# A residual moved into the sum over experts, and a multiplication by gamma moved to GpSimd

## What is computed

```python
mixed = jnp.einsum('bnsed,bnse->bnsd', out.reshape(b, nh, s, ne, d), gs)
resid = sx[jnp.arange(nh), jnp.arange(nh)]
hn = layernorm(mixed + resid, ln_g, ln_b)
f_n = jnp.transpose(hn, (0, 2, 1, 3)).reshape(b, s, h)
fx = f_n.reshape(b, s, nh, d)
...
hx = layernorm(hx + fx, fnorm_g, fnorm_b)
fout = hx.reshape(b, s, h)
fg = jax.nn.softmax(fout @ fgate_w.T, axis=-1)
return (fout.reshape(b, s, nh, d) * fg[..., None]).reshape(b, s, h)
```

## Time and profile before

| what | value |
|---|---|
| median of 3 runs | 1426.47 us (1425.58 to 1429.7) |
| the profiled execution | 1430.59 us |
| its span in the profile | 1428.8 us |
| TensorE busy | 1322.5 us (93%) |
| VectorE busy | 1045.4 us (73%) |
| GpSimd busy | 737.2 us (52%) |
| ScalarE busy | 808.5 us (57%) |
| mean granted TensorE clock | 0.962 of full speed |

### The profile page before, as it was taken

The page is one execution under the profiler, slowest core; times in us unless marked ns, Lnnn a source line. Parts: engine busy times, 40 slices in busy tenths (PEclk is TensorE's granted clock), DMA queues, the critical chain, the costliest instruction groups (busy, mean ns, idle before and its releaser), DMA issues.

```text
span 1428.8 us, 46875 instructions
## 1 busy us (share of the span) xinstructions
PE 1322.5 (93%) x16052; PEld 944.7 (66%) x16052; DVE 1045.4 (73%) x3414; ACT 808.5 (57%) x2178; POOL 737.2 (52%) x1502
## 2 busy tenths in 40 slices
PE   1699999999899999999999999984899999999996
PEld 1455555555556666666666666653698998999996
DVE  8356766666636788888888888876577776588886
ACT  4355555555456566666666666643455454566663
POOL 6575555555424555555555555554454545455440
PEclk9999999999899999999999999995699999899998
DMA  3000000000000000000000000000000000000000
GB/s 154 1 2 1 0 0 0 0 0 0 2 1 2 2 2 0 0 0 0 0 0 0 0 0 0 0 2 1 0 1 0 0 0 1 2 7 11 5 11 13
DMA packets 6981, 7.93 MB, mean 6 GB/s; under 512 B 6272, under 2 KB 6272, under 8 KB 6784
## 3 DMA queue, kind: packets, MB, share of 16 engines
q1 hardware_dynamic: 6912, 7.02, 1.5%
HBM read 5.48 MB, written 1.54 MB: 5 GB/s over the span
## 4 chain that ended last, share of the span: by engine, by line
PE 74%; DVE 10%; issue 5%; ACT 3%; POOL 2%; DVEq 0%; ACTq 0%; POOLq 0%
PE bank_one L1397 12%; PE bank_five L954 6%; PE bank_five L1503 4%; PE bank_quad L1484 4%; PE bank_quad L1458 4%; PE bank_quad L933 3%; PE bank_pair L2290 3%; PE bank_pair L987 3%; PE bank_pair L1448 2%; PE bank_pair L1985 2%; PE bank_five L1507 2%; PE bank_quad L2280 2%; PE bank_five L1937 2%; PE bank_pair L1443 2%; PE bank_pair L1444 2%
## 5 line engine op out<-in xcount | busy, mean ns | idle before, releaser
L1382 POOL TENSOR_SCALAR_AFFINE_SELECT ex_pT<-ex_pT 128x512 f32<-128x512 f32 (+1 forms) x256 | 127.0, 519 | 178.4 <-ACT ex_pT L1623 172.0
L2360 ACT ACTIVATE mo_hT<-bank_quad,mo_b 128x188 f32<-128x188 f32 x256 | 86.1, 418 | 70.3 <-PE bank_quad L2280 70.1
L1686 DVE TENSOR_REDUCE ex_negmaxA<-bank_pair 128x4 bf16<-128x512 f32 x128 | 88.6, 692 | 32.5 <-PE bank_pair L1444 30.2
L1603 ACT ACTIVATE ex_pT<-bank_quad 128x496 f32<-128x496 f32 x128 | 74.8, 584 | 64.7 <-PE bank_quad L1487 63.7
L1924 POOL TENSOR_TENSOR ta_kk<-ta_ext 94x320 f32<-94x320 f32 x64 | 60.2, 959 | 95.2 <-DVE ta_qkn L2128 95.2
L1080 ACT ACTIVATE al_pT<-bank_quad 128x496 f32<-128x496 f32 x128 | 75.1, 588 | 49.5 <-PE bank_quad L937 49.3
L1372 POOL TENSOR_TENSOR ex_zrstd<-ex_zvar,neg_half 94x16 f32<-94x16 f32 x34 | 100.6, 2959 | 2.8
L2290 PE MATMUL bank_pair<-wsb,mo_hT 128*94 128x64 f32 x1024 | 96.0, 247 | 4.1 <-DVE mo_weighted L2422 3.3
L2290 PEld LDWEIGHTS bank_pair<-wsb,mo_hT 128*94 128x94 f32 x1024 | 90.2, 163 | 6.5 <-DVE mo_weighted L2422 4.0
L1184 DVE RECIPROCAL al_rec<-bank_five 128x188 f32<-128x188 f32 x64 | 84.7, 1323 | 3.4 <-PE bank_five L954 3.4
L862 POOL TENSOR_SCALAR_AFFINE_SELECT al_pT<-al_pT 128x512 f32<-128x512 f32 (+1 forms) x128 | 63.4, 519 | 41.0 <-ACT al_pT L1080 27.7
(11 more groups left out here) (365 smaller groups left out, 4004.2 us busy)
## 6 DMA issues: line engine op xcount, KB each, us to landing
tok_xin<-x_t SPq DMA_DIRECT2D x4, 760.0 KB, 6.9
wsb<-weights SPq DMA_DIRECT2D x1, 2308.0 KB, 13.7
out<-stream SPq DMA_DIRECT2D x16, 94.0 KB
tok_par<-tok_w SPq DMA_DIRECT2D x1, 4.5 KB, 1.6
```

The lines of the kernel that those rows point to most:

```text
L1382: nc.gpsimd.affine_select(out=view, in_=view, compare_op=ALU.is_ge, fill=0.0, base=shift, pattern=[[0, NH], [1, cols]], channel_multiplier ...
L1686: red(negmaxA[e % 2][:, D::32], R[:, 0, :].rearrange("p (n s) -> p n s", n=NH), AX.X, ALU.max, negate=True)\
L2360: nc.scalar.activation(hT[p][:, e, :], HB[e // 2 % 2][:, (e % 2) * N:(e % 2 + 1) * N], ACT.Gelu, bias=b1[:, e:e + 1]).then_inc(h_ready, 1)
```

## The change

- The constant residual is no longer a tile of its own, added each turn. The tile `mixed` gets a fifth entry beside the four experts, into which the ALiBi stage writes the residual once; the reduction L1750 sums five entries instead of four, and the addition L1764 goes, with a wait (`settle`) ahead of it.
- The multiplication by gamma moves from VectorE (L1827, behind zrstd) to GpSimd, on the centred z into a new tile `zg`, in the slot e == 3 ahead of the wait for the variance, with two waits of its own (`z_centred`; `zn_ready` of the turn before). VectorE then multiplies `zg` by zrstd and adds beta.

```diff
@@ alibi_attention
-                nc.vector.tensor_tensor(residual[:].rearrange("p h (n d) -> p n h d", n=NH),
+                nc.vector.tensor_tensor(mixed[:, :, NE].rearrange("p h n d -> p n h d"),
@@ expert_attention
-    STEPS = 19
+    STEPS = 17
...
-    mixed = sb("mixed", [P, HALVES, NE, NH, D])
+    zg = sb("zg", [P, HALVES, 2, C])
...
-                        nc.gpsimd.tensor_tensor(mixed[:, h], outs[:, h],
+                        nc.gpsimd.tensor_tensor(mixed[:, h, 0:NE], outs[:, h],
...
                 if e == 3 and valid2(r):
+                    pool.wait_ge(sem["z_centred"], r + 1)
+                    need(pool, sem["zn_ready"], r)
+                    pool.sem_inc(sem["settled"], 1)
+                    nc.gpsimd.tensor_tensor(zg[:], z[:], w("norm_g", P).rearrange("p (a c) -> p a c", a=2).unsqueeze(1)
+                                            .broadcast_to([P, HALVES, 2, C]), ALU.mult).then_inc(sem["zg_ready"], 1)
                     pool.wait_ge(sem["zvar_ready"], 2 * r + 1)
...
-            if valid(rz):
-                steps.settle()
             if valid(rn):
                 dve.wait_ge(sem["fc2_used"], rn + 1)
-            if valid(rz):
-                steps.mark(tt(z[:, :, 0, :], z[:, :, 0, :], residual[:], ALU.add))
...
                 dve.wait_ge(sem["zrstd_ready"], rz + 1)
-                link(tt(groups(z), groups(z), over_components(zrstd), ALU.mult))
-                link(tt(z[:], z[:], both("norm_g"), ALU.mult))
-                tt(zn[par][:], z[:], both("norm_b"), ALU.add).then_inc(sem["zn_ready"], 1)
+                dve.wait_ge(sem["zg_ready"], rz + 1)
+                link(tt(groups(zg), groups(zg), over_components(zrstd), ALU.mult))
+                tt(zn[par][:], zg[:], both("norm_b"), ALU.add).then_inc(sem["zn_ready"], 1)
```

More of the change, by code:

```diff
@@ L92, in build @@
         neg_half = sb("neg_half", [128, 64])
-        residual = sb("residual", [P, HALVES, C])
         w_parts = sb("w_parts", [128, 3, E * (HID + 1)], BF16)
@@ L106, in build @@
         env = dict(nc=nc, stream=stream, w=w, ident=ident, identb=identb, ones=ones,
-                   neg_half=neg_half, residual=residual, w_parts=w_parts, whole=whole, rest=rest,
+                   neg_half=neg_half, w_parts=w_parts, whole=whole, rest=rest,
                    alibi=alibi_tiles(nc, ctx), expert=expert_tiles(nc, ctx), taylor=taylor_tiles(nc, ctx),
@@ L229, in expert_tiles @@
         kT=two("kT", [128, 192]), qTb=two("qTb", [128, NE, 192], BF16), z=sb("z", [P, HALVES, 2, C]),
-        h1m=sb("h1m", [C + 1, N]), glog=sb("glog", [P, HALVES, NE + 1, NH, NE]))
+        h1m=sb("h1m", [C + 1, N]), glog=sb("glog", [P, HALVES, NE + 1, NH, NE]),
+        mixed=sb("mixed", [P, HALVES, NE + 1, NH, D]))
 def taylor_tiles(nc, ctx):
@@ L715, in alibi_attention @@
     nc, stream, w = env["nc"], env["stream"], env["w"]
-    ident, neg_half, w_parts, residual = env["ident"], env["neg_half"], env["w_parts"], env["residual"]
+    ident, neg_half, w_parts, mixed = env["ident"], env["neg_half"], env["w_parts"], env["expert"]["mixed"]
     PAIRED = QUAD // 2
@@ L1241, in expert_attention @@
     ident, identb, neg_half = env["ident"], env["identb"], env["neg_half"]
-    residual, w_parts, whole, rest = env["residual"], env["w_parts"], env["whole"], env["rest"]
-    one_row, eye, maskA, maskB, ewkb, ewqb, vals, negmaxA, negmaxB, zn, sxT, kT, qTb, z, h1m, glog = (env["expert"][n] for n in (
-        "one_row eye maskA maskB ewkb ewqb vals negmaxA negmaxB zn sxT kT qTb z h1m glog".split()))
-    STEPS = 19
+    w_parts, whole, rest = env["w_parts"], env["whole"], env["rest"]
+    one_row, eye, maskA, maskB, ewkb, ewqb, vals, negmaxA, negmaxB, zn, sxT, kT, qTb, z, h1m, glog, mixed = (env["expert"][n] for n in (
+        "one_row eye maskA maskB ewkb ewqb vals negmaxA negmaxB zn sxT kT qTb z h1m glog mixed".split()))
+    STEPS = 17
     PAIRED = NH // 2
@@ L1295, in expert_attention @@
         fg_used r_full r_used tA_full tA_used tB_full tB_used causal_done o_full o_used gate_ready gexp_ready gs_ready mixed_ready
-        z_centred sq_ready zvar_ready zrstd_ready zn_ready h1m_ready fgate_ready fexp_ready dve_step""".split()
+        z_centred zg_ready sq_ready zvar_ready zrstd_ready zn_ready h1m_ready fgate_ready fexp_ready dve_step""".split()
     sem = {n: ctx.enter_context(nc.semaphore("ex_" + n)) for n in names}
```

## The result

| what | before | after |
|---|---|---|
| median of 5 runs each | 1429.57 us (1425.58 to 1429.7) | 1435.58 us (1433.02 to 1437.12) |
| the profiled execution | 1430.59 us, span 1428.8 | 1437.12 us, span 1435.3 |
| mean granted TensorE clock | 0.962 | 0.964 |

The changed kernel is slower: the ratio is 1.0051, its 95% interval 1.0037 to 1.0065, so +7 us within +5 to +9. Single executions of the kernel before spread over 7 us (1425.2 to 1432.2 in the runs of the later comparisons, where medians of 16 to 32 of them were 1427.6 to 1428.5). The expert and mixture stretches repeat to about 0.4 us from kernel to kernel where nothing in them differs; the stretch between them doesn't.

A forecast was written before the change was run, and what follows sets the result against it. TensorE was taken to bound the expert stage's full turns. Late k fill +7.0, pair's end -1.6 and drain +0.2 gave +5.6 us on the median of 1426.47: 1432.1 us, range 1422.8 to 1436.0.

The forecast's parts named there:

- likeliest case: The forecast itself: GpSimd's gamma product holds up VectorE's product fout and TensorE loses time each turn; 1432.1 us, chance 0.50.
- The reduction's length: Expert stage, VectorE, twice a turn: summing five entries takes 0.70 us against 586 ns for four, 0.24 more a turn.
- That it hides: Full expert turns: the longer reductions cost nothing, since VectorE waits 0.37 us for TensorE soon behind them.
- the wait of 0.37 at 709.60: Full expert turn: VectorE's wait for TensorE behind the reduction and residual addition, expected to take up their delay.
- Rival D: Expert stage: the longer reduction is what costs, 0.32 a turn and +8.3 at its long end; no chance of its own.
- fout held up: Full expert turn, VectorE: the product fout waits for GpSimd's gamma multiplication and ends at 712.90 instead of 712.59, 0.31 late.
- The margin of the k fill: TensorE's k fill behind L1712: gap 0.19 less 0.15 leaves 0.04 us, so 0.27 lost a turn, +7.0 in 26 turns.
- The pair's end: End of each pair of expert turns: VectorE reaches hx earlier, 0.13 comes back in each of 12 passes, -1.6 us.
- The 0.52: Pair's end: gap from L1828's end (717.93) to L1722's start (718.45); if not a fixed time, the gain there is 0.
- zrstd to zn: Expert stage, VectorE: three instructions become two, so zn is ready 0.45 us earlier where VectorE bounds it.
- the 0.34: Pair's end: how much earlier VectorE gets there, instead of 0.45, if GpSimd's late selection holds L1826 up.
- The drain: Behind turn 32, beside the first Taylor turns: shorter norm against blocked small product and late selections, +0.2 us, ends -1.8 and +1.5.

## Why the prediction was right and wrong

It said slower, and 1435.58 lies at the very end of its range (1422.8 to 1436.0), outside the likeliest case's own (1429.5 to 1434.5). The 1432.1 is 3.5 too low, and the nearness of the +5.6 to the measured +6.0 is chance: one term was three times too large, and two that weigh as much were missing.

- **The reduction's length: right.** 0.70 forecast, 0.694 measured. **That it hides: wrong, and the step that failed.** I followed the end of the reductions along z alone, to the wait of 0.37 at 709.60. But the gate's maximum and subtraction stand behind them on VectorE, and on these hangs the release of bank_one for b01, 0.20 behind, with no slack. Rival D had the price (0.32 a turn, +8.3 at its long end) and I dismissed it with that 0.37. It is 0.14 a turn, +3.3. Here the path was wrong, not only a size.
- **fout held up: right in kind.** GpSimd's product comes first, and the tail behind its end is 0.14 (0.15 forecast). The product stood 0.31 ahead of fout and not 0.20, since it needs not wait as L1369 did: it starts 0.97 behind the start of the selections, where L1369 started 1.08 behind. So fout is 0.19 late, not 0.31.
- **The margin of the k fill: wrong**, at the place I had called the weakest. It rested on 0.15 from turn 33, where TensorE had been idle for 0.86. The clock isn't the reason: it was 1.00 there, and at 0.50, later in the drain of the kernel before, the gap is the same:

```profile
966.40 0.41 DVE L1712 TENSOR_TENSOR ex_outs<-bank_one,ex_rec 94x256 f32<-94x256 f32 x1
...
966.95 0.96 PE L1397 MATMUL bank_one<-ex_znT,wsb 128*128 128x188 f32 x2 [1.23 <-DVE ex_outs L1712]
```

In the full turn TensorE isn't idle (the product ahead, L1468, starts 0.12 before the fill), and it follows L1717 after 0.06; the margin was 0.13, not 0.04. The loss a turn is 0.06 to 0.09, and the term +2.4 in place of +7.0. Of the 0.21 too much a turn, 0.09 is this margin and 0.12 the lateness of fout above.
- **The pair's end: right in kind, too small.** The 0.52 is not a fixed time from the last VectorE instruction; hx now starts 0.03 behind fc2. 0.21 in each of 12 passes, -2.5 in place of -1.6.
- **zrstd to zn**: one instruction less, but in full turns the scaling itself is held up by the late selections, 0.53 instead of 0.42, the pair of the earlier trace rows again; the 0.34 had allowed for it.
- **The drain**: L1788 at 0.56 is the blocked small product that I put at 0.42; drain and Taylor together +0.2, as forecast. That is one pair of executions in a stretch that varies by up to 5, so it bears the forecast out weakly.
- **The mixture: not thought of.** +2.5, from where its loop stands in VectorE's program.
- **The base**: the median of three that was shown, 1426.47, lies 3.1 below that of the five, 1429.57. Against the latter the same sum would have read 1435.2, close for the wrong reasons.

## What to carry to other kernels

When an instruction on a busy engine gets longer, list every semaphore that is raised behind it until the engine's next wait; a wait further on takes up the delay only for what stands behind that wait. Measure a hand-over with the engine in the state in which it will be used: 0.15 for a TensorE that had been idle was 0.06 for one that was at work, and the 0.09 was nearly half of what the term had too much. And when a change's losses appear in a stage it doesn't touch, compare the places of that stage's loops in each engine's program before looking for anything deeper.

## What the hardware did that I had not expected

- The idle time of VectorE behind a loop's branch back is 0.16 or 0.28 us in the same code, by where the loop begins in its program (1345, 1347, 1363 against 1327, 1329, 1331), and in the mixture that was worth 2.5 us in 183, about half of it through a cast that it pushed into GpSimd's way.
- A GpSimd fill of 94x512, which only writes, doesn't hold up a VectorE product of two SBUF operands (0.28 inside it); a GpSimd product does, until 0.14 to 0.15 behind its end for 128 elements, the selections until 0.26 behind theirs for 256, and the power of 94x16 doesn't.
- TensorE's fill starts 0.06 behind the end of L1717 when TensorE was at work until then, and 0.15 behind it (L1712) when it had been idle, at a granted clock of 1.00 and of 0.50 alike. At the b01 fill, where a wait and a separate semaphore increment stand between, it is 0.20.
- 20 semaphore increments in a row took VectorE 1.8 us, 0.09 each.
